# Blank rows behind each expert's last token instead of zeroing the whole slot table, pieces of 64 rows, and a loop body of 8 experts

## The reference, cut to what matters

```python
scores = jax.nn.softmax(x @ gate_w.T, axis=-1)
topk_w, topk_idx = jax.lax.top_k(scores, 6)
C = 2 * ((N * 6 + E - 1) // E)                     # 384 slots per expert
buf = zeros((E, C, D)).at[se, pos_c].add(...)      # tokens gathered by expert
g = einsum('ecd,efd->ecf', buf, w_gate)
u = einsum('ecd,efd->ecf', buf, w_up)
eo = einsum('ecf,edf->ecd', silu(g) * u, w_down)
y = zeros_like(x).at[st].add(eo[se, pos_c] * weight) + shared(hidden_states)
```

## Time and profile before

| | |
|---|---|
| median of 3 runs | 620.96 us (616.93 to 621.48) |
| profiled execution, its own time | 624.11 us |
| its span, first to last instruction | 622.4 us |
| TensorE busy | 508.2 us, 82% |
| granted TensorE clock, mean | 0.937 |
| from the first instruction to the first expert's matmul | 270.3 us |
| the 64 steps, first matmul to last | about 328 us |
| from there to the end | about 24 us |
| HBM | 81.18 MB read, 63.83 MB written |

### The profile page before, as it was taken

How to read it: one execution, slowest core, us unless ns; L and a number is a source line. 1 busy time by engine, 2 the same in 40 slices (tenths; PEclk the granted TensorE clock), 3 DMA queues, 4 the chain that set the end, 5 groups by cost and what they waited for, 6 DMA issues and landing times.

```text
span 622.4 us, 11506 instructions
## 1 busy us (share of the span) xinstructions
PE 508.2 (82%) x2483; PEld 364.2 (59%) x2484; DVE 313.9 (50%) x823; ACT 188.1 (30%) x398; POOL 330.0 (53%) x289
## 2 busy tenths in 40 slices
PE   0797299489899899979999879999789898999920
PEld 0443153253545355558888757788668776889710
DVE  8731164274866862254445526555265544555424
ACT  0111012011221211033444425454255444455410
POOL 8900050572474767603767635655465545656750
PEclk9997689689999999989999979999799999999975
DMA  6999999996794222238999969999699989899779
GB/s 205 365 390 393 358 393 404 392 363 212 239 309 143 110 84 112 101 98 212 234 231 227 238 134 219 229 213 252 148 205 239 249 220 229 196 243 227 146 148 307
DMA packets 92394, 146.55 MB, mean 235 GB/s; under 512 B 10824, under 2 KB 72120, under 8 KB 92280
## 3 DMA queue, kind: packets, MB, share of 16 engines
q1 hardware_dynamic: 61608, 83.30, 42.6%
q0 software_dynamic: 30672, 61.75, 38.5%
HBM read 81.18 MB, written 63.83 MB: 233 GB/s over the span
## 4 chain that ended last, share of the span: by engine, by line
PE 49%; SPq 19%; DMA 10%; issue 10%; DVE 7%; POOL 3%; ACT 1%; POOLq 0%; DVEq 0%
PE bank L1074 21%; PE bank L1095 7%; PE bank L1096 7%; SPq L356 5%; SPq L355 5%; DMA x_g<-in_x 4%; PE bank L1055 4%; POOL slot_rows L491 3%; PE bank L935 2%; DMA wt<-in_wdt 2%; SPq L392 2%; PE bank L885 2%; SPq L363 2%; DVE M L749 1%; PE bank L956 1%
## 5 line engine op out<-in xcount | busy, mean ns | idle before, releaser
L502 POOL DMA_INDIRECT acc<-sil,sids x64 | 99.3, 1552 | 89.2 <-ACT sil L597 57.8
L491 POOL DMA_INDIRECT slot_rows<-ctok,sli x96 | 95.2, 991 | 80.0 <-issue 27.7
L502 POOL DMA_INDIRECT acc<-OH,sids x63 | 97.6, 1549 | 53.6 <-ACT OH L597 19.3
L1074 PE MATMUL bank<-xgT,wb 128*128 128x192 f32 (+9 forms) x384 | 85.2, 375 | 15.1 <-issue 12.8
L1074 PEld LDWEIGHTS bank<-xgT,wb 128*128 128x128 f32 (+1 forms) x384 | 65.6, 198 | 29.2 <-issue 17.0
L1096 PE MATMUL bank<-wt,hh 128*128 128x256 f32 x254 | 75.5, 379 | 0.0
L849 DVE TENSOR_TENSOR hh<-sg,bank 48x384 f32<-48x384 f32 x64 | 35.6, 556 | 74.0 <-ACT sg L586 73.2
L1096 PEld LDWEIGHTS bank<-wt,hh 128*128 128x128 f32 x254 | 48.3, 190 | 6.6
L584 ACT ACTIVATE sg<-bank 128x384 f32<-128x384 f32 x64 | 31.4, 491 | 55.4 <-PE bank L1074 55.1
L597 ACT ACTIVATE sil<-bank,wcol 128x256 f32<-128x256 f32 x64 | 29.7, 474 | 53.1 <-PE bank L1096 51.7
L597 ACT ACTIVATE OH<-bank,wcol 128x256 f32<-128x256 f32 x64 | 29.8, 474 | 51.3 <-PE bank L1096 50.0
(11 more groups left out here) (185 smaller groups left out, 739.1 us busy)
## 6 DMA issues: line engine op xcount, KB each, us to landing
cw<-slot_rows SPq DMA_DIRECT2D x127, 136.0 KB
cw<-in_cW SPq DMA_DIRECT2D x64, 256.0 KB, 6.2
wb<-in_wblk SPq DMA_DIRECT2D x32, 496.0 KB, 4.1
slot_rows<-xgT POOLq DMA_DIRECT2D x12, 1088.0 KB, 15.9
slot_rows<-wb POOLq DMA_DIRECT2D x12, 1088.0 KB, 25.0
h0T<-in_wblk SPq DMA_DIRECT2D x16, 496.0 KB
hT<-in_wblk SPq DMA_DIRECT2D x16, 496.0 KB
acc<-zrow POOLq DMA_DIRECT2D x2, 2432.0 KB
```

The lines of the kernel that those rows point to most:

```text
L491: pool.indirect_dma_start(slots_d, bass.IndirectOffsetOnAxis(sli[:, g % 2, k, t:t + 1], 0), ctok[:, g % 2, t, :], None, bounds_check=SLOTS ...
L502: pool.indirect_dma_start(acc[u % 2], bass.IndirectOffsetOnAxis(sids[:, u % SR, j:j + 1], 0), yo[u % UE][:, j, :], None, compute_op=ALU.ad ...
L1074: ins = mm(bank[o][0:m, 0:n], w(b, c), xgT[u % UE][:, c, 0:n], start=c == 0, stop=c == DC - 1)
```

## The change

The advance filling goes: its 24 DMAs, their wait and the blocks of 16 rows. Each expert now has 384 + 64 rows in one piece (`SPACED`), and once the counts are known SP writes one piece of 64 blank rows behind each expert's last used slot (`fill`, with a register for its place). The first eight are written before the loop, then one per step, and the rows of an expert are loaded only after its fill has landed. DVE computes the place of each fill and loses two operations of each group's slot numbers.

Sizes go in steps of 64 (six classes from 64 to 384), and row loads, transposes, down matmuls and the adding DMAs take 128 rows and, where the count says so, 64 in the last piece. All of them now branch by `by_rows` over six variants. The loop body holds 8 steps and runs seven times; one step stands ahead of it, 7 behind it.

```diff
-RB = 16
-SLOTS = E * CAP
+H = P // 2
+SPACED = CAP + H
+SLOTS = E * SPACED
-UL = 16
+UL = 8
 LOOPS = E // UL - 1
-SIZES = [P, 3 * P // 2, 2 * P, 5 * P // 2, CAP]
+AHEAD = 1
+SIZES = [n * H for n in range(1, CAP // H + 1)]
...
-        def by_tiles(eng, size, work):
-            with eng.If(size > THREE):
-                work(3)
-            with eng.Else():
-                with eng.If(size > TWO):
-                    work(2)
-                with eng.Else():
-                    work(1)
+        def by_rows(eng, size, work, lo=0, hi=len(SIZES)):
+            if hi - lo == 1:
+                work(SIZES[lo])
+                return
+            mid = (lo + hi) // 2
+            with eng.If(size > mid - 1):
+                by_rows(eng, size, work, mid, hi)
+            with eng.Else():
+                by_rows(eng, size, work, lo, mid)
+
+        def parts(n):
+            return [(j, min(P, n - j * P)) for j in range((n + P - 1) // P)]
...
+            def fill(e, u):
+                sp.dma_start(slots_d[bass.ds(get(UNUSED, e, u), H), :], blank[:, :]).then_inc(s_unused[u % SR], 16)
+
+            for e in range(UE + 3 + AHEAD):
+                fill(e, e)
             for q in range(2):
                 sp.wait_ge(s_scat[q], 16 * TOPK * TG * G // 2)
...
-                load(0)
-                with sp.If(size > TWO):
-                    load(1)
-                    with sp.If(size > THREE):
-                        load(2)
+                sp.wait_ge(s_unused[u % SR], (16 // SR) * (e - u % SR + SR))
+                sp.sem_inc(s_tick, 1)
+                by_rows(sp, size, load)
...
                 if not (isinstance(e, int) and e >= E - UE - 3):
+                    if not (isinstance(e, int) and e >= E - UE - 3 - AHEAD):
+                        fill(e + UE + 3 + AHEAD, u + UE + 3 + AHEAD)
                     rows_free(e + 3)
                     loads(e + UE + 3, u + UE + 3)
...
-            pool.wait_ge(s_w, 16 * 8)
-            for b in range(CAP // RB):
-                pool.dma_start(slots_d[b * E * RB:(b + 1) * E * RB, :].rearrange("(n p) c -> p n c", p=P),
-                               blanks[b % len(blanks)].unsqueeze(1).to_broadcast([P, E * RB // P, RW])).then_inc(s_init, 16)
...
-            pool.wait_ge(s_init, 16 * CAP // RB)
...
-                scatter(0)
-                pool.wait_ge(s_ys, 2 * e + 3)
-                pool.wait_ge(s_yv, e + 2)
-                pool.sem_inc(s_tick, 1)
-                with pool.If(size > TWO):
-                    scatter(1)
-                    with pool.If(size > THREE):
-                        scatter(2)
+                by_rows(pool, size, scatter)
...
-                link(v.tensor_scalar(blk[:, :], blk[:, :], 1.5 * 2 ** 23, 1.5 * 2 ** 23, ALU.add, ALU.subtract))
-                link(v.scalar_tensor_tensor(sc[:, :], blk[:, :], float((E - 1) * RB), sc[:, :], ALU.mult, ALU.add))
...
                     for c in range(DC):
-                        for j in range(tiles):
-                            last = tr(bank[c][:, j * P:(j + 1) * P], xg[:, u % UE, j, c * P:(c + 1) * P], ident[:, :])
+                        for j, rows in parts(n):
+                            last = tr(bank[c][:, j * P:j * P + rows], xg[0:rows, u % UE, j, c * P:(c + 1) * P], ident[0:rows, 0:rows])
...
-                by_tiles(pe, get(SIZE, e, u), work)
+                by_rows(pe, get(SIZE, e, u), work)
```

More of the change, by code:

```diff
@@ L91, in program @@
         zrow = sb("zrow", [P, D])
+        blank = sb("blank", [H, RW])
         i_q0 = sb("i_q0", [P, TT], I32)
@@ L223, in program @@
         s_ws = sem("shared_weights_loaded")
-        s_init = sem("slot_tokens_initialised")
+        s_unused = [sem(f"unused_slots_filled{i}") for i in range(SR)]
         s_x = sem("x_loaded")
@@ L441, in _ @@
             pool.memset(onesb[:, :], 1.0)
-            for blank in blanks:
-                pool.memset(blank, 0.0)
-            pool.iota(e_off_i[:, :], [[RB, E]], base=0, channel_multiplier=0)
+            pool.memset(blank[:, :], 0.0)
+            pool.iota(e_off_i[:, :], [[SPACED, E]], base=0, channel_multiplier=0)
             pool.iota(iota_i[:, :], [[1, E]], base=0, channel_multiplier=0)
@@ L458, in _ @@
                                pattern=[[-3, K0], [0, R0]], channel_multiplier=1)
-            for b, blank in enumerate(blanks):
-                last = pool.iota(blank[:, TOK:TOK + 1].bitcast(I32), [[0, 1]], base=N + b * RB, channel_multiplier=1)
-            last.then_inc(s_const, 1)
+            pool.iota(blank[:, TOK:TOK + 1].bitcast(I32), [[0, 1]], base=N, channel_multiplier=1).then_inc(s_const, 1)
             pool.wait_ge(s_const, 3)
@@ L779, in group @@
                     for i, n in enumerate(SIZES[:-1]):
[L780 removed]
+                        v.tensor_scalar(more[:, i, :], bank[6][:, 0:E], n + 0.5, None, ALU.is_ge)
+                    last = v.tensor_scalar(unused[:, :], bank[6][:, 0:E], float(CAP), None, ALU.min)
                     last.then_inc(s_fl, 1)
@@ L1046, in tokens, with work @@
             def tokens(e, u):
[L1048 to L1052, removed]
+                def work(n):
                     for c in range(DC):
-                        for j in range(tiles):
-                            last = tr(bank[c][:, j * P:(j + 1) * P], xg[:, u % UE, j, c * P:(c + 1) * P], ident[:, :])
+                        for j, rows in parts(n):
+                            last = tr(bank[c][:, j * P:j * P + rows], xg[0:rows, u % UE, j, c * P:(c + 1) * P], ident[0:rows, 0:rows])
                         last.then_inc(s_xp, 1)
                 gathered = get(GATHERED, e, u)
-                by_tiles(pe, get(SIZE, e, u), work)
+                size = get(SIZE, e, u)
+                pe.wait_ge(s_xg[u % UE], gathered)
+                if u:
+                    pe.wait_ge(s_xs, e)
+                    pe.wait_ge(s_xv, e)
+                pe.sem_inc(s_tick, 1)
+                by_rows(pe, size, work)
             def step(e, u, first=False):
@@ L1084, in down, with work @@
             def down(e, u):
-                def work(tiles):
+                def work(n):
                     if u == E - 1:
@@ L1091, in work @@
                     pe.wait_ge(s_yv, e + 1)
[L1092 to L1096, removed]
-                        if j != 2:
[L1098 to L1111, removed]
+                    order = [parts(n)[i] for i in (0, 2, 1) if i < len(parts(n))]
+                    for j, rows in order:
+                        o = bank[5 + j][0:rows, 0:D]
+                        mm(o, hh[:, u % 2, 0, j * P:j * P + rows], down_first(u % UE), start=True, stop=False)
+                        last = mm(o, hh[:, u % 2, 1, j * P:j * P + rows], wt[u % UE], start=False, stop=True)
+                        if j != 2:
+                            last.then_inc(s_dp, 2 if len(order) == 1 else 1)
+                by_rows(pe, get(SIZE, e, u), work)
             pe.wait_ge(s_flags, 1)
```

34 lines of the change are left out of this document (18 added, 16 removed).

## The result

The changed kernel takes **690.36 us** (median of 4 runs, 690.0 to 700.86), the kernel before 618.94 us (4 runs) beside it: ratio 1.116, 95% interval 1.106 to 1.126. That is 71 us slower. The forecast was 654 us, 33 slower. The direction holds, and the wide range of 606 to 695 us takes the result in; the forecast's own range, 635 to 680 us, does not, and the loss is more than twice the one forecast.

A forecast was written before the change was run, and what follows sets the result against it. Transfers bound the first half of the first part, TensorE the rest. From 624.1 us profiled, -33.4 (filling) +29 (branches back) +13 (longer ways) +24 (code fetch) gave 656.7, or 654 us against the median; range 635 to 680, wide 606 to 695.

The forecast's parts named there:

- First part, -33.4: Groups before the experts: without the advance filling they start 36.5 us apart throughout, -33.4 us, bounded by -21 and -38.
- What it adds, 1: branches back: TensorE's loop end: four more branches back at about 7.2 us each, half-clock matmuls included, +29 us (+14 to +34).
- What it adds, 2: longer ways: TensorE's branchings for classes 128 and 192: more compares and a semaphore step, 0.4 us per expert, +13 us (0 to +15).
- What it adds, 3: code to be fetched: TensorE's sequencer in the steps: 93 block entries instead of 60, skipped code fetched too, waits for blocks +24 us.
- SP, 5.6 us per step, covered: SP's step with the fill: about 5.6 us for two pieces, 341 us if SP alone decided, covered by the slower steps.
- Sum: Whole kernel: 624.1 - 33.4 + 29 + 13 + 24 = 656.7 us profiled, 654 us against the median.
- blocks arrive in time: TensorE's code fetch keeps up; only branches back and longer ways count, 630 us; chance 0.14.
- faster: The steps keep their 328 us or cost +14 or less, as emptier DMA queues speed fetches; 588 to 610 us; chance 0.15.
- Starved throughout: Every code block in TensorE's steps costs about a branch back's 5.1 us: 93 x 4.7 = 437 us, 697 in all; chance 0.10.

The follow-up runs named there:

- before_ul8: Kernel before with loops of 8 experts instead of 16, nothing else changed; 743.23 us, ratio 1.058 to the kernel before, steps 364.0 us.
- compact_act: Changed kernel with TensorE's variants as few as before and blank rows issued by ACT instead of SP; 634.04 us, ratio 1.019, steps 371.4 us.
- best16: Changed kernel with TensorE's variants as few as before, blank rows issued by ACT, loops of 16; 591.68 us, ratio 0.953, steps 325.6 us.
- after_ul16: Changed kernel with loops of 16 experts again, everything else kept; 756.74 us, ratio 1.078 to the kernel before, steps 399.2 us.
- before_pad: Kernel before plus 29 never-executed matmuls (116 TensorE instructions) per step that every expert jumps over; 772.55 us, ratio 1.102, steps 391.3 us.
- The two doses: Kernel before with 29 or 15 skipped matmuls (116 or 60 instructions) per step; ratios 1.102 and 1.042, steps 391.3 and 350.1 us.
- after_act: Changed kernel, loops of 8 and all variants kept, blank rows issued by ACT instead of SP; 694.17 us, ratio 1.117, steps 431.0 us.
- best_unrolled: Changed kernel with TensorE's variants as few as before, blank rows issued by ACT, 64 steps written out; 566.58 us, ratio 0.912, steps 299.2 us.
- before_unrolled: Kernel before with its 64 steps written out and nothing else changed; 674.01 us, ratio 0.966, steps 299.7 us.
- after_unrolled: Changed kernel with its 64 steps written out; 732.24 us, ratio 1.048 to the kernel before, steps 374.1 us.

## Why the prediction was right in direction and wrong in size

By its own steps:

- **First part, -33.4: right.** -31.9 where the shared expert ends. On the two other chips it was less: 22 to 27 us in the first set and 10 to 14 in the third, by the first gate and up.
- **"What it adds, 1: branches back", +29: right here, 26.7** (425.9 against 399.2), but with luck. In kernels whose blocks are otherwise in time four more cost 38 us (before_ul8) and 46 us (compact_act against best16), 9.4 to 11.4 each where I had 7.2: the sum of branch and half clock lacks the second late block, which stood at three of the four added ones in both. In the changed kernel a part of that was already paid for.
- **"What it adds, 2: longer ways", +13: 7.9 us together with the smaller pieces.** after_ul16 and before_pad have the same code length and loops, and their steps differ by 7.9 us, in which all else of the change lies too; how much the ways take of it no run shows. What I had wrong is that the smaller pieces cost the array at most 0.1 us per expert: the transposes alone take 0.5 us more, and in all they are most of some 30 us of matmul time. Behind late blocks little of that shows. What the pieces cost with short code was not run.
- **"What it adds, 3: code to be fetched", +24: this is the step that failed. It is 65 us** (before_pad against the kernel before), and 74 us together with the longer ways and the smaller pieces (after_ul16 against best16). The mechanism was the named one: blocks, skipped code included, 99 packets for 29 matmuls that never run. What failed is how it was sized. I took 4.0 us per entry as the average that the steps had, let half of the entries come 0.8 us early, and subtracted. But the slack of a slow step is not carried over: only the next block is under way, so a step of class 320 that leaves 6 us for a block that takes 4 gives nothing to the two steps of class 192 behind it, which each stand for theirs. The two doses show that curve. And I priced the waits alone; of before_pad's 65 us, 19 are matmuls that take longer, up to 15 of them by the clock behind the gaps.
- **SP, 5.6 us per step, covered: right.** 5.66 measured for two pieces, and after_act did not gain from relieving it. Uncovered it binds at 358 us, where I had put 341.
- **Sum.** 326.4 + 65 + 8 + 27 = 426 for the steps, with -32 ahead of them and -1 behind: +67, against 66 between the two spans and 71 between the medians. This sum has to come out: 65, 8 and 27 are the differences along one row of kernels, from the one before over before_pad and after_ul16 to the changed one. In another order the parts differ, since a wait for one thing hides another: the same four branches back are 27 us at the end of the row and 38 at its start.

Of the rivals, "blocks arrive in time" and "faster" are dead by before_pad. "Starved throughout", 437 us for the steps and 697 in all, came nearer to 426 and 690 than the forecast did. Its price of 4.7 us for each of 93 entries stands beside 425.9 / 93 = 4.58; the bulk of the steps was on that side of the curve already, and 0.10 was too little for it.

The Trainium skill, "Runtime: NRT & Kernel Launch", section "Instruction fetch mechanics", calls the crossing of a block "mostly hidden" and, of branches, says that kernels prefer full unrolling. The trace of best_unrolled agrees with the first, 5.3 us per packet and 10 us idle in all its steps; before_pad, at 4.3 us per packet, differs from it by 65 us, and the measurement decides. The second the runs confirm, 26.4 us from best16 to best_unrolled.

Two things stay open. One is why the loop costs 26 to 27 us when only two branches back go. The four steps at them account for 15.7 of the 26.7 us in before_unrolled; the rest lies spread over the other steps and was not taken apart. The other is what the pieces of 64 rows, or the longer ways, cost where TensorE's code is short: every run that has them on TensorE has the long code too.

## What to carry to other kernels

Count the instructions that a sequencer passes per step, skipped variants included, and the blocks that these make. Compare each short step, not the average step, with the time of a block: here waits in a row ended 3.5 to 5 us apart, and a block is some 240 instructions. A finer case distinction that saves little arithmetic is paid for by every path that skips it; look also at whether its smaller pieces are faster at all, here they were slower. Unroll where the loop is not needed, and put a new small DMA per step on the queue that has air.

## What the runs showed of the hardware

- Branches back were dear on TensorE alone: 4.2 to 5.2 us in the changed kernel, where DVE's, ACT's, POOL's and SP's took 34 to 67 ns each in the same loop.
- A block's own transfer is short: 1.2% of 16 engines' 688.5 us for 107 packets is 1.2 us each. The waits do not look like a lack of bandwidth: they grew while the DMA share fell from 0.89 to 0.71.
- A long branch of TensorE ended 1.0 to 1.6 us after a 16 KB packet of code had ended, each of 46 in before_pad.
- Four transposes of which two have 64 rows took longer than four of 128 rows: 0.93 us to the next gate and up instead of 0.43 (after_unrolled and before_unrolled).
- On the chip of the first set TensorE stood still in a group while POOL sent its 24 indirect DMAs. In after_ul16 SP's next condition matrices were issued over 28 us, one instruction in 0.7 us, and ACT and PE stood as follows (timelines):

```profile
122.63 0.60 ACT L537 ACTIVATE h0T<-bank 128x512 f32<-128x512 f32 x1 [13.31 <-remote]
123.55 1.22 PE L902 MATMUL bank<-h0T,W1s 128*128 128x512 f32 x1 [25.79 <-DVE h0T L620]
```

POOL's own DMAs took their usual 0.98 us. The changed kernel on its chip shows none of this at the same place, and no run here tells what differs.
